# An edge sort in which GpSimd makes the maximum of half of each step's pairs

## The chip, the core and the metric

The kernel runs on one core of one Trainium2 chip. The metric is the device time of one execution in microseconds (us). The kernel before takes 11703.05 us in the median of 3 runs (11698.67 to 11715.26).

## The reference

The reference is a network of four layers on x of shape (8, 128, 64, 64): an involution (a 7x7 filter computed from the data), a mixture of 8 experts with a capacity, a 3x3 convolution, and a mixture of 4 experts whose gates come from a graph attention over 524288 random edges and one loop for each node. Only the last needs the sort:

```
src = edge_index[0] and the loops;  dst = edge_index[1] and the loops
e = leaky_relu(a_src[src] + a_dst[dst], negative_slope=0.2)
e_max = segment_max(e, dst);  ee = exp(e - e_max[dst])
denom = segment_sum(ee, dst)
agg = segment_sum(h[src] * (ee / (denom[dst] + 1e-16))[:, :, None], dst)
```

To make the segment sums into scans, the kernel first sorts the 524288 edges by destination. The key of an edge is the whole number (dst + 256) shifted left by 15, or'ed with src: the destination above, the source in the 15 bits below.

## The kernel before

`metaformer` runs its stages one after the other, each in a block of its own with a barrier at its end: the sort of the edges, the involution with the first routing, the experts, the node ranges, the convolution, the scan over the edges, and the gates with the output. Every stage starts when all engines have left the one before.

`sort_edges` (L1085 to L1234) is a bitonic sorting network. The keys lie as 128 partitions x 4096 in one of two buffers, `buf[0]` and `buf[1]`; each step reads one and writes the other, and `a` says which is read. A key is compared as the fp32 number whose bits it is, which for positive numbers orders in the same way as the whole numbers. The list `steps` (L1104 to L1112) is made beforehand and walked in order (L1188 to L1222). It has these kinds:

- "both", 66 steps (runs shorter than 4096): pairs lie `d = 1 << j` apart, and blocks go up and down by turns. Four instructions on VectorE, each on 1024 elements a partition: minimum and maximum for the blocks that go up (`e = 0`), and for those that go down (`e = 1`), where the two outputs change places (L1216, L1217).
- "rows", 124 steps (longer runs, all in one direction): two instructions on VectorE, the minimum and the maximum of all 2048 pairs (L1210, L1211).
- "sign", 8 steps: partitions that go down are multiplied by -1 (L1205, L1207).
- "turn", 14 steps: the keys are transposed in blocks on TensorE into PSUM, and ScalarE and VectorE copy them back (L1158, L1166, L1195), so that pairs that lie in different partitions come to lie in one.

After the last instruction of a step VectorE waits for the semaphore `stage` to reach the step's number (L1219 to L1221), because the next step reads what this one wrote. In a turn VectorE raises `turn_in` (L1192), for which TensorE waits. GpSimd's part of this stage is a single iota (L1145). At the end VectorE takes the keys apart into sources, destinations and a mark for equal neighbours, and SyncE stores them.

Other lines that the text speaks of: L388 is a copy on GpSimd in the involution, beside which VectorE makes one-hot rows (L204, L205); L1760 are GpSimd's indirect DMAs in the last stage, beside which VectorE multiplies and adds (L1847, L1854, L1858, L1866); L92, L94 and L739 are memsets on GpSimd.

Of the kernel before, what the change touches and what calls it, by code (L numbers as in the profile page):

```python
# [50 lines left out]
FE = NEDGE // P  # L51
# [1033 lines left out]
def sort_edges(nc, src, dst, srcs, dsts, cont, ident):  # L1085
# [3 lines left out]
    with ExitStack() as ctx:  # L1089
# [6 lines left out]
        sign = sb("sign", [P, LP + 1])  # L1096
        loaded, made, stage = sem("loaded"), sem("made"), sem("stage")
        turn_in, turn_psum, turn_act, turn_dve = sem("turn_in"), sem("turn_psum"), sem("turn_act"), sem("turn_dve")
        done, stored = sem("done"), sem("stored")


# [19 lines left out]
        def bank_dst(t, q):  # L1121
# [4 lines left out]
                return out.rearrange("p (q b) -> p b q", b=FE // P)[:, 4 * q:4 * q + 4]  # L1126
            return out.rearrange("q (b p) -> q b p", p=P)[:, 4 * q:4 * q + 4]

        block = ctx.enter_context(nc.Block())

        @block.sync
# [11 lines left out]
        @block.gpsimd  # L1143
        def _(pool):
            nc.gpsimd.iota(part[:], pattern=[[0, 1]], base=0, channel_multiplier=1).then_inc(made, 1)  # L1145

        @block.tensor
        def _(pe):
# [21 lines left out]
        def _(dve):  # L1170
# [12 lines left out]
            dve.wait_ge(stage, 3 + LP)  # L1183
            nc.vector.tensor_scalar(sign[:, 0:LP], bit[:], -2.0, 1.0, ALU.mult, ALU.add)
            nc.vector.memset(sign[:, LP:LP + 1], 1.0).then_inc(stage, 1)
            n, t, a = 4 + LP, 0, 0
            dve.wait_ge(stage, n)
            for kind, k, j in steps:  # L1188
                x, y = buf[a][:], buf[1 - a][:]
                d = 1 << j  # L1190
                if kind == "turn":
                    dve.sem_inc(turn_in, 1)  # L1192
                    for q in range(1, NTURN, 2):
                        dve.wait_ge(turn_psum, NTURN * t + q + 1)
                        nc.vector.tensor_copy(bank_dst(t, q), bank[q][:].rearrange("p (b q) -> p b q", b=4)  # L1195
                                              ).then_inc(turn_dve, 1)
                    t += 1
                    dve.wait_ge(turn_act, (NTURN // 2) * t)
                    dve.wait_ge(turn_dve, (NTURN // 2) * t)
                    a ^= 1  # L1200
                    continue
                if kind == "sign":
                    m = k - LF
                    if m == 0:
                        ins = nc.vector.tensor_scalar(y, x, sign[:, 0:1], None, ALU.mult)  # L1205
                    else:
                        ins = nc.vector.tensor_scalar(y, x, sign[:, m - 1:m], sign[:, m:m + 1], ALU.mult, ALU.mult)  # L1207
                elif kind == "rows":
                    vx, vy = (v.rearrange("p (m two d) -> p m two d", two=2, d=d) for v in (x, y))
                    nc.vector.tensor_tensor(vy[:, :, 0], vx[:, :, 0], vx[:, :, 1], ALU.min)  # L1210
                    ins = nc.vector.tensor_tensor(vy[:, :, 1], vx[:, :, 0], vx[:, :, 1], ALU.max)  # L1211
                else:
                    vx, vy = (v.rearrange("p (n e m two d) -> p n e m two d", e=2, two=2, d=d, m=1 << (k - j - 1))
                              for v in (x, y))
                    for e in range(2):
                        nc.vector.tensor_tensor(vy[:, :, e, :, e], vx[:, :, e, :, 0], vx[:, :, e, :, 1], ALU.min)  # L1216
                        ins = nc.vector.tensor_tensor(vy[:, :, e, :, 1 - e], vx[:, :, e, :, 0], vx[:, :, e, :, 1],  # L1217
                                                      ALU.max)
                ins.then_inc(stage, 1)  # L1219
                n += 1  # L1220
                dve.wait_ge(stage, n)  # L1221
                a ^= 1  # L1222
            key = fin[:].bitcast(I32)
            nc.vector.tensor_scalar(other[:].bitcast(I32), key, (1 << 15) - 1, None, ALU.bitwise_and).then_inc(done, 1)
# [6 lines left out]
            nc.vector.memset(other[:, 0:1], 0.0)  # L1231
            nc.vector.tensor_tensor(other[:, 1:FE], key[:, 1:FE], key[:, 0:FE - 1], ALU.is_equal).then_inc(done, 1)

        return loaded, made, stage, turn_in, turn_psum, turn_act, turn_dve, done, stored  # L1234


def node_ranges(nc, counts, ends, endtab, ident):
# [809 lines left out]
```

## Time and profile before

| | us |
|---|---|
| median of 3 runs | 11703.05 |
| lowest, highest | 11698.67, 11715.26 |
| the profiled execution | 11711.42 |
| its span, first to last instruction | 11709.7 |
| busy: TensorE, VectorE, ScalarE, GpSimd | 5363.1, 4831.0, 2011.8, 5292.8 |
| the sorting network, steps alone | 24.47 to 1015.10 of the span |

The profile is of one execution, on the one core. DVE is VectorE, POOL is GpSimd, ACT is ScalarE, PE is TensorE's matmuls and PEld its weight loads, SP is SyncE. A queue is named by a q behind the engine. A timeline line has the start in us from the span's start, the duration in us, the engine, the line of the kernel, the operation, output <- input and their shapes, and in brackets the engine's idle time before it with what released it. Durations of neighbours on one engine overlap a little, so the distance of two starts is the better measure of a sequence. A waiting engine whose instruction has already been handed over shows the wait as part of that instruction's duration, not as idle time.

### The profile page before, as it was taken

The page shows a single profiled execution, that of the slowest core. Times are in us where ns is not written, and L with a number is a line of the kernel's source. Part 1 is how long each engine was busy: PE and PEld are TensorE (multiplying, and loading weights), DVE is VectorE, ACT ScalarE, POOL GpSimd, SP SyncE. Part 2 cuts the span into 40 slices and gives each one's busy share as a digit, 9 for nine tenths or more (in the row PEclk, how much of TensorE's full clock was granted, in tenths as well). Part 3 has the DMA queues.
Part 4 walks back from the last instruction along what each step waited for, and adds up shares of the span by engine and source line. Part 5 has one row for each costly group of instructions (what it writes and reads, how often), then busy time and mean ns, then how long its engine had stood idle before and what let it go on. Part 6 is the DMA issues. An engine that isn't in the chain of part 4 may idle for free. (4 is left out here: it accounts for less than half of the span.)

```text
span 11709.7 us, 84534 instructions
## 1 busy us (share of the span) xinstructions
PE 5363.1 (46%) x20795; PEld 3127.3 (27%) x20795; DVE 4831.0 (41%) x13362; ACT 2011.8 (17%) x3739; POOL 5292.8 (45%) x5293
## 2 busy tenths in 40 slices
PE   0112999999978996888512112121212122121135
PEld 0111666666656772333200000000000000000012
DVE  9996666666657873434211111111111111111168
ACT  0000333333322321111011111111111111111100
POOL 0000111111110004333477777777777777777662
PEclk9755999999989998888756555565556565565568
DMA  0002000000002112332411111111111111111165
GB/s 14 0 0 101 23 23 23 22 21 21 20 19 89 57 52 51 56 58 59 51 34 36 33 36 35 35 39 31 39 32 39 33 36 34 36 39 31 39 168 190
DMA packets 382082, 514.68 MB, mean 44 GB/s; under 512 B 215894, under 2 KB 302735, under 8 KB 357139
## 3 DMA queue, kind: packets, MB, share of 16 engines
q1 hardware_dynamic: 184466, 260.41, 7.9%
q0 software_dynamic: 164992, 77.85, 6.8%
q10 hardware_dynamic: 32256, 171.98, 3.7%
q8 instruction: 175, 2.87, 0.1%
q14 instruction: 193, 1.57, 0.0%
HBM read 249.78 MB, written 263.86 MB: 44 GB/s over the span
## 5 line engine op out<-in xcount | busy, mean ns | idle before, releaser
L1501 POOL DMA_INDIRECT e_row<-rows_dram,e_idx x4096 | 4031.5, 984 | 1264.4 <-issue 1264.4
L1447 PE MATMUL e_bank<-e_hid,e_w 128*128 128x512 f32 x1024 | 592.9, 714 | 4189.1 <-ACT e_hid L1477 4189.1
L1534 DVE COPY e_idx<-e_allidx 128x64 int32 x64 | 13.2, 206 | 4353.4 <-DMA e_row<-rows_dram,e_idx 4353.4
L1447 PEld LDWEIGHTS e_bank<-e_hid,e_w 128*128 128x128 f32 x1024 | 220.7, 223 | 4492.4 <-issue 4492.4
L388 POOL COPY a_xc<-a_xp 128x1573 f32<-128x1573 f32 x104 | 167.7, 1617 | 1224.2 <-PE a_bank L441 1111.7
L205 DVE TENSOR_SCALAR a_cnta_hot<-a_cnta_iota,a_cnta_part 128x256 bf16<-128x256 bf16 x2368 | 693.1, 293 | 0.0
L1485 ACT ACTIVATE e_ex<-e_dx 128x512 f32<-128x512 f32 x64 | 40.3, 630 | 3573.7 <-DVEq L1547 3573.7
L204 DVE TENSOR_SCALAR a_cnta_hot<-a_cnta_iota,a_cnta_part 128x128 bf16<-128x128 bf16 x2368 | 649.6, 274 | 0.0
L397 POOL DMA_INDIRECT xb_dram<-a_so,a_sidx x256 | 251.4, 982 | 813.5 <-DVE a_sidx L664 548.1
L467 PE MATMUL a_bank<-a_taps,a_xt 121*128 121x100 f32 x2704 | 590.9, 360 | 2.0 <-ACT a_xt L531 2.0
L951 POOL DMA_INDIRECT v_dram<-c_td,c_fidx x256 | 251.4, 982 | 736.4 <-DVE c_td L1076 660.8
L1440 PE MATMUL e_bank<-e_h,e_w 128*128 128x512 f32 x1024 | 509.7, 627 | 67.8 <-DMA e_h<-hn_dram 67.8
L980 PE MATMUL c_bank<-c_xp,c_w 128*128 128x512 f32 x1152 | 497.8, 593 | 19.0 <-ACT c_rl L1005 19.0
L429 PE MATMUL a_bank<-a_hid,a_canvas 128*121 128x169 f32 x1600 | 484.1, 481 | 6.9 <-ACT a_hid L517 6.9
L1158 PE MATMUL s_bank<-keep_ident,s_keys 128*128 128x128 f32 x448 | 83.6, 373 | 876.0 <-DVEq L1192 876.0
L205 DVE TENSOR_SCALAR b_cntb_hot<-b_cntb_iota,b_cntb_part 128x256 bf16<-128x256 bf16 x1728 | 481.9, 279 | 0.3 <-issue 0.3
L367 POOL MEMSET a_xp<- 128x5041 f32 x1 | 4.3, 4301 | 1038.3 <-POOLq L1992 1038.3
L467 PEld LDWEIGHTS a_bank<-a_taps,a_xt 121*128 121x128 f32 x2704 | 452.8, 200 | 11.4 <-ACT a_xt L531 3.6
L204 DVE TENSOR_SCALAR b_cntb_hot<-b_cntb_iota,b_cntb_part 128x128 bf16<-128x128 bf16 x1728 | 427.3, 247 | 0.1
L212 PE MATMUL a_bank<-a_cnta_hot 128*128 128x256 bf16 x2368 | 401.6, 275 | 16.3 <-DVE a_cnta_hot L205 1.9
L1263 POOL MEMSET h_ones<- 128x128 f32 x1 | 0.2, 206 | 863.8 <-POOLq L675 863.8
L429 PEld LDWEIGHTS a_bank<-a_hid,a_canvas 128*121 128x121 f32 x1600 | 330.7, 207 | 162.9 <-ACT a_hid L517 14.2
(345 smaller groups left out, 10655.0 us busy)
## 6 DMA issues: line engine op xcount, KB each, us to landing
e_row<-rows_dram,e_idx POOLq DMA_INDIRECT x4096
ys_dram<-e_y ACTq DMA_DIRECT2D x64, 1024.0 KB, 4.0
f_ye<-ys_dram SPq DMA_DIRECT2D x64, 1024.0 KB, 4.8
res_dram<-e_st ACTq DMA_DIRECT2D x64, 768.0 KB, 3.3
xb_dram<-a_taps SPq DMA_DIRECT2D x4, 5120.0 KB, 31.1
b_tok<-xb_dram SPq DMA_DIRECT2D x80, 256.0 KB, 2.7
yb_dram<-b_y ACTq DMA_DIRECT2D x80, 256.0 KB, 2.0
x_dram<-a_xs SPq DMA_DIRECT2D x9, 2048.0 KB, 6.3
```

The lines of the kernel that those rows point to most:

```text
L204: self.nc.vector.tensor_scalar(h[:, 0:P], self.iota[:, 0:P], self.part[:, 0, c:c + 1], None, ALU.is_equal)
L205: self.nc.vector.tensor_scalar(h[:, P:], self.iota[:], self.part[:, 1, c:c + 1], None, ALU.is_equal).then_inc(self.hot_ready, 1)
L212: self.nc.tensor.matmul(self.psum, h[:, 0:P], h[:, P:], start=(c == 0), stop=(c == self.C - 1)).then_inc(self.counted, 1)
L388: nc.gpsimd.tensor_copy(xq[a % 2].rearrange("p (b r c) -> p b r c", r=IN, c=IN), bass.AP(tensor=rows.tensor, offset=rows.offset, ap=[list( ...
L397: nc.gpsimd.indirect_dma_start(xb, bass.IndirectOffsetOnAxis(ap=sidx[:, t:t + 1], axis=0), ht[:, t], None, bounds_check=SLOTS - 1, oob_is_ ...
L429: nc_mm = nc.tensor.matmul(bank[q % 4][0:KIN, (z % 3) * NP:(z % 3 + 1) * NP], canvas[:, g, at:at + KIN], hid[:, r::OUT, c::OUT], start=Tru ...
L467: mm = nc.tensor.matmul(bank[6 + v % 2][:, (b - b0) * G * NOUT:(b - b0 + 1) * G * NOUT], xt[0:KIN, u % 3, z % 4, :], taps[0:KIN, :, z], st ...
L951: nc.gpsimd.indirect_dma_start(v, bass.IndirectOffsetOnAxis(ap=fidx[:, t:t + 1], axis=0), td[:, t], None, bounds_check=NEDGE - 1, oob_is_e ...
L980: mm = nc.tensor.matmul(bank[4 + t % 2][:], w9[:, k], xp[:, 8 * t + a:8 * t + a + 8, b:b + W], start=(k == 0), stop=(k == K3 * K3 - 1))
L1440: nc.tensor.matmul(bank[m % UPB][:], w1[:, e, f * P:(f + 1) * P], h[:, s], start=True, stop=True).then_inc(up_psum, 1)
L1447: mm = nc.tensor.matmul(bank[UPB + n % DNB][:], w2[:, n % NE, f], hid[:, n % 2, f], start=(f == 0), stop=(f == NF1 - 1))
L1501: nc.gpsimd.indirect_dma_start(row[:, s, u], None, rows, bass.IndirectOffsetOnAxis(ap=idx[:, s, u:u + 1], axis=0)).then_inc(gath[s], 16)
```

## The change

The pairs of every "rows" and "both" step are cut into two halves of 1024 pairs a partition by the new function `halves`. For "both" the halves are the blocks that go up and those that go down; for "rows" they are the first and second half of the runs, or, where there is one run alone, of its elements. VectorE makes minimum and maximum of the first half as before, and the minimum alone of the second. GpSimd makes the maximum of the second half in two instructions on the keys as whole numbers: the sum of both inputs, written where the maximum belongs, and then that sum less the minimum.

Four semaphores order this. VectorE raises `input_ready` at the start of a step, and GpSimd's sum waits for it. The minimum of GpSimd's half is VectorE's first instruction of the step and raises `least_ready`. GpSimd's difference waits for its own sum (`mixed`) and for `least_ready`, and raises `maxed`. At the end of a step VectorE waits for `maxed` as well as for `stage`. Signs, turns and what comes before and after the network stay as they are.

```
--- before.py
+++ after.py
@@ -1096,6 +1096,7 @@
         sign = sb("sign", [P, LP + 1])
         loaded, made, stage = sem("loaded"), sem("made"), sem("stage")
         turn_in, turn_psum, turn_act, turn_dve = sem("turn_in"), sem("turn_psum"), sem("turn_act"), sem("turn_dve")
+        input_ready, least_ready, mixed, maxed = (sem(n) for n in ("input_ready", "least_ready", "mixed", "maxed"))
         done, stored = sem("done"), sem("stored")
 
 
@@ -1126,6 +1127,18 @@
                 return out.rearrange("p (q b) -> p b q", b=FE // P)[:, 4 * q:4 * q + 4]
             return out.rearrange("q (b p) -> q b p", p=P)[:, 4 * q:4 * q + 4]
 
+        def halves(x, k, j, kind):
+
+            d = 1 << j
+            if kind == "rows":
+                vx = x.rearrange("p (m two d) -> p m two d", two=2, d=d)
+                m = FE // (2 * d)
+                cut = [(slice(0, m // 2), slice(0, d)), (slice(m // 2, m), slice(0, d))] if m > 1 else [
+                    (slice(0, 1), slice(0, d // 2)), (slice(0, 1), slice(d // 2, d))]
+                return [[(vx[:, a, 0, b], vx[:, a, 1, b])] for a, b in cut]
+            vx = x.rearrange("p (n e m two d) -> p n e m two d", e=2, two=2, d=d, m=1 << (k - j - 1))
+            return [[(vx[:, :, e, :, 0], vx[:, :, e, :, 1])] for e in range(2)]
+
         block = ctx.enter_context(nc.Block())
 
         @block.sync
@@ -1143,6 +1156,19 @@
         @block.gpsimd
         def _(pool):
             nc.gpsimd.iota(part[:], pattern=[[0, 1]], base=0, channel_multiplier=1).then_inc(made, 1)
+            n, a = 0, 0
+            for kind, k, j in steps:
+                if kind in ("rows", "both"):
+                    n += 1
+                    pool.wait_ge(input_ready, n)
+                    (x,), (y,) = halves(buf[a][:], k, j, kind)[1], halves(buf[1 - a][:], k, j, kind)[1]
+                    least, most = (v.bitcast(I32) for v in (y[::-1] if kind == "both" else y))
+                    nc.gpsimd.tensor_tensor(most, x[0].bitcast(I32), x[1].bitcast(I32), ALU.add
+                                            ).then_inc(mixed, 1)
+                    pool.wait_ge(mixed, n)
+                    pool.wait_ge(least_ready, n)
+                    nc.gpsimd.tensor_tensor(most, most, least, ALU.subtract).then_inc(maxed, 1)
+                a ^= 1
 
         @block.tensor
         def _(pe):
@@ -1183,7 +1209,7 @@
             dve.wait_ge(stage, 3 + LP)
             nc.vector.tensor_scalar(sign[:, 0:LP], bit[:], -2.0, 1.0, ALU.mult, ALU.add)
             nc.vector.memset(sign[:, LP:LP + 1], 1.0).then_inc(stage, 1)
-            n, t, a = 4 + LP, 0, 0
+            n, t, a, pooled = 4 + LP, 0, 0, 0
             dve.wait_ge(stage, n)
             for kind, k, j in steps:
                 x, y = buf[a][:], buf[1 - a][:]
@@ -1205,20 +1231,18 @@
                         ins = nc.vector.tensor_scalar(y, x, sign[:, 0:1], None, ALU.mult)
                     else:
                         ins = nc.vector.tensor_scalar(y, x, sign[:, m - 1:m], sign[:, m:m + 1], ALU.mult, ALU.mult)
-                elif kind == "rows":
-                    vx, vy = (v.rearrange("p (m two d) -> p m two d", two=2, d=d) for v in (x, y))
-                    nc.vector.tensor_tensor(vy[:, :, 0], vx[:, :, 0], vx[:, :, 1], ALU.min)
-                    ins = nc.vector.tensor_tensor(vy[:, :, 1], vx[:, :, 0], vx[:, :, 1], ALU.max)
                 else:
-                    vx, vy = (v.rearrange("p (n e m two d) -> p n e m two d", e=2, two=2, d=d, m=1 << (k - j - 1))
-                              for v in (x, y))
-                    for e in range(2):
-                        nc.vector.tensor_tensor(vy[:, :, e, :, e], vx[:, :, e, :, 0], vx[:, :, e, :, 1], ALU.min)
-                        ins = nc.vector.tensor_tensor(vy[:, :, e, :, 1 - e], vx[:, :, e, :, 0], vx[:, :, e, :, 1],
-                                                      ALU.max)
+                    dve.sem_inc(input_ready, 1)
+                    pooled += 1
+                    px, py = halves(x, k, j, kind), halves(y, k, j, kind)
+                    nc.vector.tensor_tensor(py[1][0][kind == "both"], px[1][0][0], px[1][0][1], ALU.min
+                                            ).then_inc(least_ready, 1)
+                    nc.vector.tensor_tensor(py[0][0][0], px[0][0][0], px[0][0][1], ALU.min)
+                    ins = nc.vector.tensor_tensor(py[0][0][1], px[0][0][0], px[0][0][1], ALU.max)
                 ins.then_inc(stage, 1)
                 n += 1
                 dve.wait_ge(stage, n)
+                dve.wait_ge(maxed, pooled)
                 a ^= 1
             key = fin[:].bitcast(I32)
             nc.vector.tensor_scalar(other[:].bitcast(I32), key, (1 << 15) - 1, None, ALU.bitwise_and).then_inc(done, 1)
@@ -1231,7 +1255,7 @@
             nc.vector.memset(other[:, 0:1], 0.0)
             nc.vector.tensor_tensor(other[:, 1:FE], key[:, 1:FE], key[:, 0:FE - 1], ALU.is_equal).then_inc(done, 1)
 
-        return loaded, made, stage, turn_in, turn_psum, turn_act, turn_dve, done, stored
+        return loaded, made, stage, turn_in, turn_psum, turn_act, turn_dve, input_ready, least_ready, mixed, maxed, done, stored
 
 
 def node_ranges(nc, counts, ends, endtab, ident):
```

## Rows read from the trace of the kernel before

**Rows 1.** The page: engines (part 1), two lines of the slices (part 2).

```profile
PE 5363.1 (46%) x20795; PEld 3127.3 (27%) x20795; DVE 4831.0 (41%) x13362; ACT 2011.8 (17%) x3739; POOL 5292.8 (45%) x5293
...
DVE  9996666666657873434211111111111111111168
...
POOL 0000111111110004333477777777777777777662
```

**Rows 2.** Busy time by stretch: length, each engine's busy us, clock, DMA.

```profile
24.47:332.60 308.13, 0.00 (x0) 0.00 (x0) 305.92 (x262) 0.00 (x0) 0.00 (x0) 1.00 0.00 0
332.60:1015.10 682.50, 83.61 (x448) 80.62 (x448) 626.21 (x316) 44.59 (x56) 0.00 (x0) 0.60 0.00 0
```

**Rows 3.** Timeline (start, duration, engine, line) at the next stage's start.

```profile
1040.53 4.30 POOL L367 MEMSET a_xp<- 128x5041 f32 x1 [1038.27 <-POOLq L1992]
```

**Rows 4.** Groups by line in the sort: count, busy us, mean ns, idle before.

```profile
L1210 DVE TENSOR_TENSOR s_keys<-s_keys 128x2048 f32<-128x2048 f32 x124 | 284.2, 2292 | 5.4
...
L1216 DVE TENSOR_TENSOR s_keys<-s_keys 128x1024 f32<-128x1024 f32 x132 | 162.7, 1233 | 2.3
```

**Rows 5.** Timeline in the sort: first step, a "both" and a "rows" step.

```profile
24.47 2.00 DVE L1216 TENSOR_TENSOR s_keys<-s_keys 128x1024 f32<-128x1024 f32 x1
...
32.14 1.23 DVE L1216 TENSOR_TENSOR s_keys<-s_keys 128x1024 f32<-128x1024 f32 x1
...
36.80 1.23 DVE L1216 TENSOR_TENSOR s_keys<-s_keys 128x1024 f32<-128x1024 f32 x1
37.95 1.22 DVE L1217 TENSOR_TENSOR s_keys<-s_keys 128x1024 f32<-128x1024 f32 x1
...
41.47 1.22 DVE L1216 TENSOR_TENSOR s_keys<-s_keys 128x1024 f32<-128x1024 f32 x1
...
416.36 2.29 DVE L1210 TENSOR_TENSOR s_keys<-s_keys 128x2048 f32<-128x2048 f32 x1
...
420.89 2.29 DVE L1210 TENSOR_TENSOR s_keys<-s_keys 128x2048 f32<-128x2048 f32 x1
```

**Rows 6.** Timeline of GpSimd at the start: a wait on itself.

```profile
1.26 0.29 POOL L1982 TENSOR_SCALAR_AFFINE_SELECT keep_ident<-keep_ident 128x128 f32<-128x128 f32 x1 [0.24 <-POOL keep_ident L1980]
```

**Rows 7.** GpSimd's groups by line, and the copy's min/median/max.

```profile
L739 POOL MEMSET b_zeros<- 128x4096 f32 x1 | 3.5, 3507 | 0.0
...
L92 POOL MEMSET keep_ln_ones<- 128x128 f32 x1 | 0.2, 207 | 0.0
...
L388 POOL COPY a_xc<-a_xp x104: 1542/1612/1695, 1148.2 to 3369.4; 128x1573 f32<-128x1573 f32 x104
```

**Rows 8.** Timeline around a copy on GpSimd, and min/median/max of L204.

```profile
1229.99 1.59 DVE L204 TENSOR_SCALAR a_cnta_hot<-a_cnta_iota,a_cnta_part 128x128 bf16<-128x128 bf16 x1
...
1229.88 1.66 POOL L388 COPY a_xc<-a_xp 128x1573 f32<-128x1573 f32 x1 [6.50 <-PE a_bank L441]
...
L204 DVE TENSOR_SCALAR a_cnta_hot<-a_cnta_iota,a_cnta_part x2368: 235/242/1618, 1216.5 to 3393.2; 128x128 bf16<-128x128 bf16 x198
```

**Rows 9.** Timeline of the last stage, and min/median/max of L1760.

```profile
11331.55 1.43 POOL L1760 DMA_INDIRECT f_st<-res_dram,keep_last_i  x1 [0.30 <-issue]
...
11332.08 1.21 DVE L1847 TENSOR_TENSOR f_prod<-f_ye,f_wide 128x1024 f32<-128x1024 f32 x1
...
11333.28 2.56 POOL L1760 DMA_INDIRECT f_st<-res_dram,keep_last_i  x1 [0.30 <-issue]
...
11333.81 1.21 DVE L1854 TENSOR_TENSOR f_acc<-f_prod 128x1024 f32<-128x1024 f32 x1
...
11334.95 1.21 DVE L1847 TENSOR_TENSOR f_prod<-f_ye,f_wide 128x1024 f32<-128x1024 f32 x1
...
L1760 POOL DMA_INDIRECT f_st<-res_dram,keep_last_i x256: 940/945/2566, 11117.0 to 11561.8; - x128
```

**Rows 10.** Timeline: GpSimd released by VectorE.

```profile
1147.29 0.69 DVE L149 TENSOR_TENSOR a_xp<-a_xc,a_bank 128x512 f32<-128x512 f32 x1 [0.17 <-PE a_bank L122]
...
1148.17 1.55 POOL L388 COPY a_xc<-a_xp 128x1573 f32<-128x1573 f32 x1 [99.14 <-DVE a_xp L149]
```

## The prediction

> **What bounds the kernel now.** The page comes first: one core, GpSimd, TensorE and VectorE each busy under half of the span [rows 1], so no engine bounds the whole; the kernel is a row of stages with barriers between them. The slices of the page show which stage the change meets: in slices 0 to 2 VectorE stands at 9 tenths and GpSimd at 0 [rows 1]. The table of busy time by stretch gives the stage its edges: 24.47 to 1015.10 us is the sorting network, first 308.13 us in which VectorE alone works, then 682.50 us in which TensorE and ScalarE help at the turns; GpSimd is at 0.00 in both [rows 2]. The next stage starts on GpSimd after 1038.27 us of idle [rows 3], so what the network gains or loses moves all that follows by the same amount. Nothing after it overlaps it.
>
> Inside the network VectorE is its own bound. The groups by line show 124 "rows" steps of two instructions of 2048 elements, and 66 "both" steps of four instructions of 1024 [rows 4]. The instructions overlap a little at their ends, so I go by starts in the timeline. A "both" step takes 41.47 - 36.80 = 4.67 us, and within it one instruction follows the next by 1.14 us [rows 5]. Four times 1.14 are 4.56, so the wait between steps costs 0.11 us. A "rows" step takes 420.89 - 416.36 = 4.53 us [rows 5]. The very first step, whose elements lie 16 bytes apart, takes 32.14 - 24.47 = 7.67 us [rows 5].
>
> **The change part by part.** Of every step VectorE now issues three instructions of 1024 elements: the minimum of GpSimd's pairs, then the minimum and maximum of its own. GpSimd issues two, a sum and a difference, on 1024 elements each. The three on VectorE cost 3 x 1.14 = 3.42 us, plus the 0.11 us of the wait, plus a semaphore increment and a second wait. The trace doesn't price these two alone; they lie between nothing and GpSimd's 0.24 us for a wait on itself [rows 6], and I take 0.05 us, as they are nearer to VectorE's own wait. VectorE's share of a step is thus 3.58 us: 0.95 us less in "rows", 1.09 us less in "both".
>
> GpSimd has no two-input instruction in this trace, so its price is bounded. Its copies of 1573 elements have a median of 1612 ns [rows 7], 1.025 ns an element; a memset of 4096 takes 3507 ns [rows 7], 0.85 ns an element; one of 128 takes 207 ns, of which 0.1 us doesn't go with the elements [rows 7]. If two inputs cost no more than one, an instruction takes 1024 x 1.025 + 0.1 = 1.15 us. If each input is a pass of its own, it takes 2.2 us at the copy's rate and 1.84 us at the memset's. If the result is a third pass, it takes 3.25 us. I take 2.2 us: the copy is the nearest row, since it reads and writes as these do, and the doubled input is the one difference.
>
> The Trainium skill ("GPSIMD Engine Reference", section "Elementwise — side-by-side cycle accounting") puts a GpSimd tensor_tensor of 2048 fp32 elements at 4497 ns, because both inputs share one read port; no run here shows it. Half of it is an estimate of 2.25 us, by which the forecast below would be some 20 us later.
>
> Does GpSimd's work lie beside VectorE's, or behind it? Two sets of rows speak. First, while GpSimd copied from 1229.88 for 1.66 us, a VectorE instruction of 0.24 us in the median took 1.59 us and ended with the copy, at 1231.58 against 1231.54 [rows 8]. VectorE was held for GpSimd's whole instruction. Second, in the last stage VectorE runs two-input instructions of the same kind and size as the sort's, back to back, and GpSimd's indirect DMAs, 945 ns in the median, take 1.43 and 2.56 us [rows 9]. Each ends 0.9 us after one of VectorE's starts: 11331.55 + 1.43 is 0.90 behind 11332.08, and 11333.28 + 2.56 is 0.89 behind 11334.95 [rows 9]. GpSimd was held until a VectorE instruction gave way. What isn't shown is a two-input VectorE instruction against a GpSimd instruction that reads all the time; both halves of an exclusive hold are. So I take the step's five instructions as one queue, not two.
>
> The Trainium skill says the same of the pair that isn't shown ("SBUF — State Buffer", section "Who interferes with whom": a two-input VectorE instruction against a GpSimd read, the later one blocks entirely). By it the forecast stands; without it the no-hold rival below would have more weight.
>
> The queue has two possible orders. VectorE goes first, since GpSimd is released by a VectorE event only 0.2 us later (1148.17 against 1147.29 + 0.69) [rows 10]. If the two then take turns, the step is 3.58 + 2 x (2.2 - 0.2) = 7.58 us: the held VectorE instruction of [rows 8] ended 0.04 us after the copy though it needs 0.24 us, so 0.2 us overlap at each handover. The wait between sum and difference is covered by VectorE's instruction. If VectorE runs its three first (a waiting GpSimd let one of VectorE's starts, 11333.81, go by [rows 9]), the step is 3.42 + 2.2 + 0.24 + 2.2 + 0.11 + 0.05 = 8.22 us, with GpSimd's release of VectorE put at the 0.11 us of VectorE's wait on itself. I take the middle, 7.9 us, since the rows don't tell the order.
>
> Behind the new wait on VectorE stands the next step's whole work, and, at the 14 turns, the increment that lets TensorE begin; nobody else waits. Signs, turns and the code behind the sort are untouched and GpSimd sits idle in them. Clearing four more semaphores on SyncE costs well under 1 us.
>
> The sum: 124 x (7.9 - 4.53) = 418 us; 65 x (7.9 - 4.67) = 210 us; the first step 3 x 1.9 + 0.16 + 4.4 = 10.3 against 7.67, 3 us. Together +631 us. On the median, 11703 + 631 = **12334 us**; the profiled execution (11711.4 us, 1.7 of it around the span) would read 12342. That is 5.4% slower. A difference of 0.2%, 23 us, is about what a measurement of this kernel can tell from no change.
>
> **The rivals.**
> 1. The hold is shared element by element. Then VectorE's second inputs (3 x 1024 at 1.1 ns, 3.4 us) and GpSimd's inputs (4 x 1024 at 0.85 ns, 3.5 us) queue at one port, and the step is about 7.0 us: 124 x 2.47 + 65 x 2.33 = +458, 12161 us. For it: nothing in the rows; against it, the hold of a whole copy [rows 8].
> 2. Hold, but cheap GpSimd instructions (1.15 us): 3.58 + 2 x 0.95 = 5.48 us a step, 118 + 53, about 11874 us. No row shows a second input for nothing.
> 3. No hold between these two kinds, GpSimd's chain sets the step: 0.2 + 2.2 + 0.24 + 2.2 + 0.11 = 4.95 us, 124 x 0.42 + 65 x 0.28 - 2 = +68, 11771 us. For it: the rows that hold VectorE are of a one-input form. Against it: [rows 9], where the two-input form holds GpSimd.
> 4. The other side, faster: no hold and GpSimd hidden. VectorE's three instructions set the step at 3.58 us, 124 x 0.95 + 65 x 1.09 + 2 = 191 us off, 11512 us. It decides only if there is no hold and a GpSimd instruction takes under 2.0 us, where 0.55 + 2A passes a step of 4.57 us. With a hold, a gain would need A under 0.7 us, less than one pass over 1024 elements.
> 5. The change doesn't do what it says: the whole-number sum is rounded and the keys come out other than the maxima. The instructions and their durations stay; only the addresses of later gathers would differ. No time of its own follows; with whatever else could keep the step as it is, the result is near 11703 us.
>
> **How the numbers follow.** Full hold with two passes or more: 0.77. Shared element by element: 0.07. Hold, cheap instructions: 0.04. No hold, GpSimd's chain: 0.06. No hold, hidden: 0.03. The fifth: 0.03, mostly within 0.2%. The range: its low end is the full hold at the memset's rate, taking turns: 3.58 + 2 x 1.64 = 6.86 us, 289 + 142 + 2, about 12136 us, rounded to 12130, which takes in rival 1. Its high end is three passes, taking turns: 3.58 + 2 x 3.05 = 9.68 us, 639 + 326 + 4, 12672 us, rounded to 12670; 0.04 of the first case lies above it (three passes, VectorE first). So 0.80 lies inside. Faster by over 0.2%: 0.03; within: 0.02; slower: 0.95.
>
> **What would show each step.** Full hold: in the sort, VectorE's 1024-element instructions no longer all take 1.22 us [rows 5]; some are stretched by a GpSimd instruction, or GpSimd's are stretched by VectorE's, and the starts of a step lie 7.6 to 8.2 us apart; the network ends near 1645 us and the next stages keep their lengths. If turns are taken, the stretched ones are VectorE's second and third; if not, VectorE's three start 1.14 us apart and GpSimd's sum is the stretched one. Price of GpSimd: the shortest distance from a sum to its difference, about 2.4 us with the wait. No hold: VectorE's durations all at 1.22 us with idle time before each step, released by GpSimd (rival 3) or none (rival 4). The prediction is wrong if the step is under 6.9 or over 9.7 us, or if time moves in a stage behind the sort.

## The result and the profile after

The changed kernel takes 12309.91 us in the median of 4 runs (12297.06 to 12317.73), the kernel before 11709.15 us in the median of 4; the ratio is 1.0515, 95% interval 1.0499 to 1.0532. That is 600.8 us more, where 631 us were forecast, and 12309.91 us lies in the forecast's range of 12130 to 12670 us. The profiled execution took 12297.06 us.

The page of the changed kernel (busy time, and the slices of VectorE and GpSimd) answers to [rows 1]:

```profile
PE 5361.0 (44%) x20795; PEld 3116.0 (25%) x20795; DVE 5405.9 (44%) x13420; ACT 2011.7 (16%) x3739; POOL 6293.1 (51%) x5673
...
DVE  9999956666666578443421111111111111111168
...
POOL 6656621111111100233347777777777777777763
```

GpSimd gained 6293.1 - 5292.8 = 1000 us of busy time, VectorE 575 us, although VectorE has one quarter fewer comparisons to make. Busy time here holds the time an instruction is held, too. Busy time by stretch answers to [rows 2]; the last line is everything behind the sort:

```profile
24.50:535.98 511.48, 0.00 (x0) 0.00 (x0) 496.12 (x198) 0.00 (x0) 350.26 (x132) 1.00 0.00 0
535.98:1615.64 1079.66, 80.36 (x448) 77.37 (x448) 1008.56 (x436) 44.61 (x56) 658.78 (x248) 0.59 0.00 0
...
1641.30:12295.30 10654.00, 5280.66 (x20347) 3038.65 (x20347) 3880.34 (x12769) 1965.79 (x3682) 5283.25 (x5286) 0.74 0.19 47
```

The network now runs from 24.50 to 1615.64 us: 1591.1 us against 990.6, which is 600.5 us more, all of the difference of the medians. What lies behind it takes 10654.0 us against 10669.2 in the execution profiled before. These 15 us are within the 21 us by which the four runs of the changed kernel differ among themselves.

The groups by line in the sort (count, busy us, mean ns, idle before) answer to [rows 4]. L1238, L1240 and L1241 are VectorE's first minimum, second minimum and maximum (in the timelines below, L1166 is GpSimd's sum and L1170 its difference):

```profile
L1238 DVE TENSOR_TENSOR s_keys<-s_keys 128x1024 f32<-128x1024 f32 x190 | 622.6, 3277 | 38.2 <-DVE s_keys L1241 31.9 <-POOL s_keys L1170 4.1 <-DVE s_keys L1231 0.2
L1241 DVE TENSOR_TENSOR s_keys<-s_keys 128x1024 f32<-128x1024 f32 x190 | 614.1, 3232 | 0.0
...
L1240 DVE TENSOR_TENSOR s_keys<-s_keys 128x1024 f32<-128x1024 f32 x190 | 231.0, 1216 | 0.0
```

Two of VectorE's three have a mean over 3.2 us, the middle one 1.22 us. One step of the timeline (start and duration in us) tells why. It answers to the steps of [rows 5]; its pairs lie 1024 elements apart:

```profile
546.50 2.34 POOL L1166 TENSOR_TENSOR s_keys<-s_keys 128x1024 int32<-128x1024 int32 x1 [1.25 <-DVEq L1235]
546.52 3.40 DVE L1238 TENSOR_TENSOR s_keys<-s_keys 128x1024 f32<-128x1024 f32 x1 [0.18 <-DVE s_keys L1241]
549.84 1.21 DVE L1240 TENSOR_TENSOR s_keys<-s_keys 128x1024 f32<-128x1024 f32 x1
550.07 3.19 POOL L1170 TENSOR_TENSOR s_keys<-s_keys 128x1024 int32<-128x1024 int32 x1 [1.23 <-DVE s_keys L1238]
550.98 3.35 DVE L1241 TENSOR_TENSOR s_keys<-s_keys 128x1024 f32<-128x1024 f32 x1
554.50 2.34 POOL L1166 TENSOR_TENSOR s_keys<-s_keys 128x1024 int32<-128x1024 int32 x1 [1.25 <-DVEq L1235]
```

The sum and the first minimum begin together, and the minimum ends 1.1 us after the sum: 546.52 + 3.40 = 549.92 against 548.84. So GpSimd was first, and VectorE did its 1.1 us of work behind it. The second minimum runs alone. The difference is handed over at 550.07 while that runs, and ends 2.2 us after the second minimum: 550.07 + 3.19 = 553.26 against 549.84 + 1.21 = 551.05. The maximum, handed over at 550.98, ends 1.07 us after the difference. Then follows 0.17 us, and the next step. All five stand in one queue, and the step takes 8.00 us. Where pairs lie 1 or 2 elements apart (50 of the 190 steps, the first among them), the sum takes 1.89 us and the step 7.11 us in all but the first:

```profile
521.90 1.89 POOL L1166 TENSOR_TENSOR s_keys<-s_keys 128x1024 int32<-128x1024 int32 x1 [1.25 <-DVEq L1235]
...
529.01 1.89 POOL L1166 TENSOR_TENSOR s_keys<-s_keys 128x1024 int32<-128x1024 int32 x1 [1.25 <-DVEq L1235]
```

The first step, with elements 16 bytes apart, went in another order. VectorE's three ran first, at 2.0 us each, and the sum was held behind all three: it took 7.71 us, where the difference behind it, with nobody beside it, took 1.98 us (32.28 to 34.26):

```profile
24.50 7.71 POOL L1166 TENSOR_TENSOR s_keys<-s_keys 128x1024 int32<-128x1024 int32 x1 [22.23 <-DVEq L1235]
...
28.28 2.06 DVE L1241 TENSOR_TENSOR s_keys<-s_keys 128x1024 f32<-128x1024 f32 x1
...
34.39 1.89 POOL L1166 TENSOR_TENSOR s_keys<-s_keys 128x1024 int32<-128x1024 int32 x1
```

### The profile page after: what moved, and what is told of

Its sections match the earlier page's. It is cut to its first block and busy times, and to the rows that moved or that the text cites. A ratio compares the mean times of both kernels' runs of the same rounds, so it can differ in the third digit from the quotient of the medians.

```text
span 12295.3 us, 85351 instructions
## 1 busy us (share of the span) xinstructions
PE 5361.0 (44%) x20795; PEld 3116.0 (25%) x20795; DVE 5405.9 (44%) x13420; ACT 2011.7 (16%) x3739; POOL 6293.1 (51%) x5673
## 5 line engine op out<-in xcount | busy, mean ns | idle before, releaser
L1170 POOL TENSOR_TENSOR s_keys<-s_keys 128x1024 int32<-128x1024 int32 x190 | 581.6, 3061 | 232.4 <-DVE s_keys L1238 232.3
L204 DVE TENSOR_SCALAR a_cnta_hot<-a_cnta_iota,a_cnta_part 128x128 bf16<-128x128 bf16 x2368 | 651.6, 275 | 0.0
L1238 DVE TENSOR_TENSOR s_keys<-s_keys 128x1024 f32<-128x1024 f32 x190 | 622.6, 3277 | 38.2 <-DVE s_keys L1241 31.9
L1166 POOL TENSOR_TENSOR s_keys<-s_keys 128x1024 int32<-128x1024 int32 x190 | 427.4, 2250 | 370.8 <-DVEq L1235 370.7
L1241 DVE TENSOR_TENSOR s_keys<-s_keys 128x1024 f32<-128x1024 f32 x190 | 614.1, 3232 | 0.0
```

Source lines behind the costliest of these rows:

```text
L204: self.nc.vector.tensor_scalar(h[:, 0:P], self.iota[:, 0:P], self.part[:, 0, c:c + 1], None, ALU.is_equal)
L1166: nc.gpsimd.tensor_tensor(most, x[0].bitcast(I32), x[1].bitcast(I32), ALU.add).then_inc(mixed, 1)
L1170: nc.gpsimd.tensor_tensor(most, most, least, ALU.subtract).then_inc(maxed, 1)
L1238: nc.vector.tensor_tensor(py[1][0][kind == "both"], px[1][0][0], px[1][0][1], ALU.min).then_inc(least_ready, 1)
L1241: ins = nc.vector.tensor_tensor(py[0][0][1], px[0][0][0], px[0][0][1], ALU.max)
```

## The experiments

The theory is the exclusive hold: a VectorE instruction with two SBUF inputs and a GpSimd instruction that reads SBUF never run at once. The rivals are a port shared element by element, a GpSimd whose chain is merely too long, and a hold of any instruction by any other. The network's length, from its first instruction to the first one behind it, serves as the measure: it is the same wherever the kernel ran. The kernels e1, e2, e3 and e9 ran on a chip on which the kernel before takes 12489.28 us in one run, where the 4096 indirect DMAs of the edge stage take 1072 ns each in the mean (profiled in e2) and not 984 ns; the unchanged network of e9_gpsimd_prices took 1591.9 us on it, against 1591.1 us.

| kernel | a step, us (pairs 4 or more apart) | network, us |
|---|---|---|
| before | 4.53 and 4.67 | 990.6 |
| changed | 8.00 | 1591.1 |
| e1, VectorE alone | 3.64 | 812.0 |
| e2, one after the other | 8.42 | 1673.7 |
| e3, second input from PSUM | 4.89 | 1049.8 |
| e4, GpSimd only writes | 3.67 | 816.1 |
| e5, GpSimd copies | 5.37 | 1146.8 |
| e8, released later | 7.82 | 1564.2 |
| e7, a quarter in "rows" alone | 6.37 ("rows") | 1204.8 |
| e10, turns compared from PSUM | 4.53 and 4.67 | 944.8 |

**VectorE alone.**

```diff
-                dve.wait_ge(maxed, pooled)
```
and GpSimd's loop over the steps taken out.

> GpSimd's sum and difference and VectorE's wait for them are taken out; VectorE keeps its three instructions of a step, so the maxima of half of the pairs are not made, and the kernel goes on with the unsorted keys, of which a copy was kept. Theory, exclusive hold (a step's five instructions stand in one queue): without GpSimd, VectorE's three all take 1.22 us and a step 3.5 to 3.6 us, the network 790 to 805 us against 990.6 before and 1591.1 in the changed kernel. Rival, something of the new order of work itself (half-size instructions, strides, the semaphore increment) is dear: VectorE's instructions stay over 1.3 us or the step over 4 us even without GpSimd.

The timeline of VectorE in the network:

```profile
503.13 1.23 DVE L1229 TENSOR_TENSOR s_keys<-s_keys 128x1024 f32<-128x1024 f32 x1
...
506.77 1.22 DVE L1229 TENSOR_TENSOR s_keys<-s_keys 128x1024 f32<-128x1024 f32 x1
```

Every instruction took 1.22 us, and a step 506.77 - 503.13 = 3.64 us. So nothing in the new order of VectorE's own work is dear, and the step of 8.00 us is GpSimd's doing. The network, 812.0 us, was a little over the expectation: between two steps lie 3.64 - 3 x 1.14 = 0.22 us, not the 0.16 us of the prediction.

**One after the other.**

```diff
-                    dve.sem_inc(input_ready, 1)
                     pooled += 1
...
                 dve.wait_ge(stage, n)
+                if kind != "sign":
+                    dve.sem_inc(input_ready, 1)
                 dve.wait_ge(maxed, pooled)
```

> GpSimd's two instructions of a step are released only when VectorE's three have ended, so that nothing overlaps; all keys are sorted. Exclusive hold: overlapping had bought next to nothing, so a step grows only by the waits and handovers, from 7.1 and 8.0 us to 7.8 and 8.7 us; GpSimd's sum and difference each take 1.9 us (pairs 1 or 2 elements apart) and 2.3 us (4 or more apart) as in the changed kernel, VectorE's three 1.22 us each; network near 1720 us. Rival, shared element by element: GpSimd alone is clearly faster than 1.9 and 2.3 us (1.2 to 1.6 us), the step 6.4 to 7.2 us. Rival, GpSimd is merely dear and VectorE's long durations are waits for data: GpSimd takes 3 us alone and the step is over 9.5 us.

The timeline of a step with pairs 1024 apart:

```profile
565.91 1.22 DVE L1237 TENSOR_TENSOR s_keys<-s_keys 128x1024 f32<-128x1024 f32 x1
...
569.55 2.34 POOL L1166 TENSOR_TENSOR s_keys<-s_keys 128x1024 int32<-128x1024 int32 x1 [6.05 <-DVEq L1245]
571.96 2.34 POOL L1170 TENSOR_TENSOR s_keys<-s_keys 128x1024 int32<-128x1024 int32 x1
574.33 1.22 DVE L1237 TENSOR_TENSOR s_keys<-s_keys 128x1024 f32<-128x1024 f32 x1 [4.92 <-POOL s_keys L1170]
```

GpSimd's two take 2.34 us each with nobody beside them, just what the sum takes in the changed kernel, and VectorE's three are back at 1.22 us. The step is 574.33 - 565.91 = 8.42 us (7.53 us for pairs 1 or 2 apart), a little under the expected 8.7 and 7.8 us, and the network took 1673.7 us where some 1720 us were expected. Running the engines together had bought 0.42 us of 8.42. That is not what a port shared element by element gives, nor did GpSimd take the 3 us of the other rival.

**The second input from PSUM.**

```diff
-px[1][0][0], px[1][0][1], ALU.min
+px[1][0][0], second, ALU.min      # second: a view of a constant PSUM tile; so for all three
```
GpSimd writes its results to a tile of its own, `apart`.

> VectorE's three instructions of a step take their second input from a constant tile in PSUM in place of SBUF, so they have one SBUF input; GpSimd's two instructions have the same forms and inputs and write to a tile of their own. The keys aren't sorted; the kernel goes on with a kept copy of them. Exclusive hold through VectorE's second SBUF input: the hold is gone, VectorE's instructions all take 1.2 to 1.3 us, GpSimd's 1.9 to 2.4 us, and a step is GpSimd's chain alone, 4.3 us (pairs 1 or 2 apart) and 5.2 us (4 or more). Rival, a hold of any VectorE instruction against any on GpSimd: stretched instructions and steps of 7.1 and 8.0 us stay.

The timeline of one step with pairs 4 apart and one with pairs 2 apart (L1171 sum, L1175 difference; L1253, L1255, L1256 VectorE):

```profile
44.07 2.31 POOL L1171 TENSOR_TENSOR s_apart<-s_keys 128x1024 int32<-128x1024 int32 x1
44.08 1.22 DVE L1253 TENSOR_TENSOR s_keys<-s_keys,s_pair 128x1024 f32<-128x1024 f32 x1 [1.49 <-POOL s_apart L1175]
...
48.90 1.89 POOL L1171 TENSOR_TENSOR s_apart<-s_keys 128x1024 int32<-128x1024 int32 x1
...
50.87 2.80 POOL L1175 TENSOR_TENSOR s_apart<-s_apart,s_keys 128x1024 int32<-128x1024 int32 x1
...
53.80 1.89 POOL L1171 TENSOR_TENSOR s_apart<-s_keys 128x1024 int32<-128x1024 int32 x1
```

VectorE's three start 1.14 us apart and take 1.22 us beside a sum of 2.31 us. The hold is gone, and the second SBUF input is what made it. The steps, 4.83 and 4.90 us, are GpSimd's chain alone (over all pairs 4 or more apart the median is 4.89 us). This is close to the prediction's third rival (4.95 us), which would have held if the two engines could run together. Both expected steps were missed. The 5.2 us for pairs 4 or more apart were 0.3 us too long. The 4.3 us for close pairs were too short, because the difference now takes 2.80 us there; its inputs lie in two tiles in this kernel, which is the likely reason, but no run varied that alone.

**GpSimd only writes, and GpSimd copies.** Two kernels, in which the sum and the difference become

```diff
+                    nc.gpsimd.memset(most, 0.0)             # e4, twice
+                    nc.gpsimd.tensor_copy(most, x[0])       # e5, then x[1]
```

> GpSimd's sum and difference are each replaced by a memset of the same 1024 elements, which reads nothing; waits and releases stay, VectorE's three instructions have two SBUF inputs as in the changed kernel. The keys aren't sorted; the kernel goes on with a kept copy. Hold by the shared reading: a memset isn't held and holds nobody; VectorE's instructions stay at 1.22 us, memsets at 0.95 us, the step at VectorE's own 3.64 us as without GpSimd. Rival, hold of any instruction by any: the memsets queue with the rest, step 3.64 + 2 x 0.95 - 0.3 = 5.2 us, with VectorE's instructions stretched to over 2 us.

> GpSimd's sum and difference are each replaced by a copy of one input, 1.07 us alone (1.11 with elements 2 apart). The keys aren't sorted; the kernel goes on with a kept copy. Exclusive hold, one queue: the changed kernel's steps fit 3.64 + 2A - 0.3 with A the price of a GpSimd instruction alone (1.89: 7.12; 2.34: 8.02), so with A = 1.07 the step is 5.5 us. Rival, the hold comes from GpSimd's two inputs and a one-input read shares the port: step 3.64 us with VectorE's durations at 1.22 us or a little more.

A step of the one with memsets:

```profile
556.16 0.95 POOL L1167 MEMSET s_keys<- 128x1024 f32 x1 [1.34 <-DVEq L1238]
556.19 1.22 DVE L1241 TENSOR_TENSOR s_keys<-s_keys 128x1024 f32<-128x1024 f32 x1 [0.17 <-DVE s_keys L1244]
...
559.83 0.95 POOL L1167 MEMSET s_keys<- 128x1024 f32 x1 [1.35 <-DVEq L1238]
```

The memsets take 0.95 us beside VectorE's 1.22 us, and nobody is held: 3.67 us a step against 3.64 without GpSimd. A step of the one with copies:

```profile
572.97 1.04 POOL L1167 COPY s_keys<-s_keys 128x1024 f32<-128x1024 f32 x1 [1.22 <-DVEq L1238]
573.00 2.09 DVE L1241 TENSOR_TENSOR s_keys<-s_keys 128x1024 f32<-128x1024 f32 x1 [0.18 <-DVE s_keys L1244]
...
576.14 2.05 DVE L1244 TENSOR_TENSOR s_keys<-s_keys 128x1024 f32<-128x1024 f32 x1
578.34 1.04 POOL L1167 COPY s_keys<-s_keys 128x1024 f32<-128x1024 f32 x1 [1.22 <-DVEq L1238]
```

Here the stretched instructions are back, with the first minimum at 2.09 us and the maximum at 2.05. The step is 5.37 us (5.46 us for close pairs), where 5.5 us were expected. So one read by GpSimd is enough, and a write is not. The Trainium skill says both ("SBUF — State Buffer", section "Who interferes with whom"), and both runs agree.

**Released later.**

```diff
-                    dve.sem_inc(input_ready, 1)
...
                     nc.vector.tensor_tensor(..., ALU.min).then_inc(least_ready, 1)
+                    dve.sem_inc(input_ready, 1)
```

> VectorE raises input_ready behind its first minimum in the program and not before it; all keys are sorted. Engines take turns at the port: GpSimd's sum, released a little later, now finds the first minimum under way and is let in either at once behind it or as before, and the step stays one queue, 7.1 and 8.0 us within 0.15 us. Rival, a VectorE that runs back to back keeps the port, as it did through the first step of the changed kernel, where the sum ended only after all three (7.71 us): the sum starts after VectorE's third, and the step takes 7.5 and 8.4 us, as with nothing overlapped.

The timeline of a step (L1237, L1240, L1241 VectorE):

```profile
549.90 1.22 DVE L1237 TENSOR_TENSOR s_keys<-s_keys 128x1024 f32<-128x1024 f32 x1
550.01 3.31 POOL L1166 TENSOR_TENSOR s_keys<-s_keys 128x1024 int32<-128x1024 int32 x1 [1.23 <-DVEq L1239]
551.04 3.36 DVE L1240 TENSOR_TENSOR s_keys<-s_keys 128x1024 f32<-128x1024 f32 x1
...
557.72 1.23 DVE L1237 TENSOR_TENSOR s_keys<-s_keys 128x1024 f32<-128x1024 f32 x1
```

Now the first minimum runs undisturbed, the sum comes in at once behind it (550.01 + 3.31 = 553.32, 2.2 us after the minimum's end), and the second minimum is the stretched one. So in this step a VectorE that runs back to back doesn't keep GpSimd out. The step is 7.82 us, 0.18 us less than in the changed kernel and a little outside the 0.15 us expected: the idle 0.18 us before VectorE's first instruction has gone. The network is 26.9 us shorter. The one execution took 12308.26 us, so this doesn't show in the total.

**A quarter for GpSimd, in "rows" steps alone.**

```diff
-                cut = [(slice(0, m // 2), slice(0, d)), (slice(m // 2, m), slice(0, d))] if m > 1 else [
+                cut = [(slice(0, m * 3 // 4), slice(0, d)), (slice(m * 3 // 4, m), slice(0, d))] if m > 3 else [
...
```
and the "both" steps as in the kernel before.

> GpSimd gets a quarter of the pairs in place of a half, and only in the 124 rows steps; the 66 both steps are those of the kernel before. All keys are sorted. Exclusive hold: GpSimd's instructions of 512 elements take 1.3 us (1.0 to 1.1 where the pairs are 1 or 2 apart), VectorE's three (512, 1536, 1536) some 3.95 us plus 0.22; the step is 4.17 + 2 x 1.3 - 0.3 = 6.5 us (5.9), worse than 4.53 before, and the network 1205 to 1225 us against 990.6 before: a smaller share only loses less. Rival, GpSimd loses by its chain being longer than VectorE's work: with a quarter, that chain of about 3 us fits behind VectorE's, and the step is 4.2 us, the network near 950 us, faster than before.

A step of the timeline:

```profile
350.59 1.26 POOL L1166 TENSOR_TENSOR s_keys<-s_keys 128x512 int32<-128x512 int32 x1 [1.78 <-DVEq L1242]
350.61 1.79 DVE L1245 TENSOR_TENSOR s_keys<-s_keys 128x512 f32<-128x512 f32 x1 [0.18 <-DVE s_keys L1248]
...
352.54 2.64 POOL L1170 TENSOR_TENSOR s_keys<-s_keys 128x512 int32<-128x512 int32 x1 [0.69 <-DVE s_keys L1245]
...
356.96 1.26 POOL L1166 TENSOR_TENSOR s_keys<-s_keys 128x512 int32<-128x512 int32 x1 [1.78 <-DVEq L1242]
```

GpSimd needs only 1.26 us for its sum, its whole chain would fit behind VectorE's 4.2 us, and still the step takes 356.96 - 350.59 = 6.37 us (5.93 us for close pairs), against 4.53 before. The execution took 11922.10 us beside 11703.22 for the kernel before. A smaller share loses less and gains nothing, which settles it against the rival of a chain that is merely too long.

**GpSimd's prices.** A row of instructions ahead of the network, while VectorE waits:

```diff
+            for d in (1, 2, 4, 8, 64, 1024):
+                run(lambda: tt(pairs(k1, d)[0], *pairs(k0, d), ALU.add))
+                run(lambda: tt(pairs(f1, d)[0], *pairs(f0, d), ALU.add))
```

> The changed kernel, with a row of GpSimd instructions ahead of the network while VectorE waits, each form twice: whole-number and fp32 sums of 1024 pairs that lie 1, 2, 4, 8, 64 and 1024 elements apart; sums with the second input 1025, 1026 and 0 elements behind the first; sums of 512 and 2048; copies and a memset of 1024. Exclusive hold: the sums cost alone what they cost in the network, 1.9 us at 1 and 2 apart and 2.3 us from 4 on, and so whatever sets these two prices is GpSimd's own and not VectorE's doing; a copy 1.1 us, a memset 0.95 us; the very first sum takes some 6 us more, as the first of the network did (7.71 us). Rival, shared: the sums are under 1.6 us alone, and both prices alike.

GpSimd's timeline; each line holds two instructions and the time of both. The first two are whole-number sums of pairs 1 and 4 apart (those 1024 apart took 4.75 us), then come a second input 1025 elements behind the first, the same input twice, and sums of 512 and of 2048:

```profile
9.24 3.86 POOL L1179 TENSOR_TENSOR s_bench<-s_bench 128x1024 int32<-128x1024 int32 x2
...
25.00 4.77 POOL L1179 TENSOR_TENSOR s_bench<-s_bench 128x1024 int32<-128x1024 int32 x2
...
63.60 4.07 POOL L1181 TENSOR_TENSOR s_bench<-s_bench 128x1024 int32<-128x1024 int32 x2
...
71.90 3.86 POOL L1183 TENSOR_TENSOR s_bench<-s_bench 128x1024 int32<-128x1024 int32 x2
75.83 2.60 POOL L1184 TENSOR_TENSOR s_bench<-s_bench 128x512 int32<-128x512 int32 x2
78.51 9.06 POOL L1185 TENSOR_TENSOR s_bench<-s_bench 128x2048 int32<-128x2048 int32 x2
```

Alone a sum takes 3.86 / 2 = 1.93 us (1 apart, and 2 apart alike) or 2.38 us (4 and 1024 apart), so both prices are GpSimd's own. The very first pair of sums took no longer than the fp32 pair behind it, 3.86 us too, so the expected 6 us for a first one were wrong: the 7.71 us of the first step were a hold, which its timeline above shows. The network behind it is the same code as the changed kernel's, and yet its first step went another way: GpSimd's sum was first, and its difference was the one that waited.

```profile
104.05 1.98 POOL L1197 TENSOR_TENSOR s_keys<-s_keys 128x1024 int32<-128x1024 int32 x1 [9.98 <-DVEq L1267]
104.06 3.77 DVE L1270 TENSOR_TENSOR s_keys<-s_keys 128x1024 f32<-128x1024 f32 x1 [0.15 <-DVE s_sign L1243]
...
107.98 5.53 POOL L1201 TENSOR_TENSOR s_keys<-s_keys 128x1024 int32<-128x1024 int32 x1 [1.95 <-DVE s_keys L1270]
```

**Turns compared straight from PSUM, without GpSimd.** As PSUM inputs cost VectorE nothing extra in e3, this one changes the kernel before: ScalarE copies the second key of each pair, and VectorE takes the first from the bank.

```diff
-                        nc.vector.tensor_copy(bank_dst(t, q), ...)
+                        nc.vector.tensor_tensor(y0, x0, z, ALU.min)
+                        nc.vector.tensor_tensor(y1, x0, z, ALU.max)
```

> The kernel before, without any work on GpSimd, and with the 14 turns changed: where it copied the transposed keys from PSUM and then ran a rows step on them, ScalarE now copies only the second key of each pair (256 elements a bank) and VectorE makes minimum and maximum straight from PSUM and that copy, 16 instructions of 256 elements a turn. All keys are sorted. What the runs so far show of the hold (one input from PSUM costs VectorE the same 1.22 us for 1024 elements and TensorE and ScalarE hold nobody) gives: a turn and the step behind it now take some 8.4 + 4.53 = 12.9 us; then 16 instructions at 0.35 to 0.4 us, 5.6 to 6.4 us, behind 2.5 us of start-up, 8 to 9 us; 14 x 4 to 5 = 55 to 70 us less, 0.5 to 0.6% faster than before. Rival, short instructions with strided PSUM inputs are dear (0.5 us or more each): a turn takes as long as before, within 0.2%.

A turn (L1173 TensorE, L1212 and L1213 VectorE from PSUM, L1226 the next step):

```profile
402.36 3.71 PE L1173 MATMUL s_bank<-keep_ident,s_keys 128*128 128x128 f32 x32 [2.08 <-DVEq L1208]
...
403.46 0.61 DVE L1212 TENSOR_TENSOR s_keys<-s_bank,s_second 128x256 f32<-128x256 f32 x1 [1.21 <-ACT s_second L1182]
...
410.69 2.29 DVE L1226 TENSOR_TENSOR s_keys<-s_keys 128x2048 f32<-128x2048 f32 x1
```

It takes 12549.78 us in the median of 6 runs, beside 12597.97 us in the median of 9 for the kernel before, measured with it (both are longer than above; in e10's profile the edge stage's indirect DMAs take 1077 ns each). The ratio is 0.9963 (0.9951 to 0.9976), so it is 0.4% faster than the kernel before, and beats both kernels; 0.5 to 0.6% were expected. The network is 45.8 us shorter, not 55 to 70. The turn with its step takes the expected 8.3 us, but those of before took 11.6 us in the mean and not 12.9: (990.6 - 124 x 4.53 - 65 x 4.67 - 7.67 - 8 x 2.4) / 14 + 4.53. Hence 3.3 us a turn and not 4 to 5.

## Why the prediction was right, step by step

- *The sort is a stage of its own, and what it loses the kernel loses.* Right: 600.5 us in the network, 600.8 us in the medians.
- *The five instructions are one queue.* Right, and shown from several sides: GpSimd's prices don't change when nothing runs beside it (e2, e9), the hold goes with VectorE's second SBUF input (e3) or with GpSimd's reading (e4), and comes back with a single read (e5). The two halves seen before, [rows 8] and [rows 9], did add up to the whole.
- *VectorE's share 3.58 us.* 3.64 us (e1); the second wait and the increment cost 0.11 us, not 0.05.
- *GpSimd's instruction 2.2 us.* The mean was right and no single one was: 1.89 us in the 50 close steps (1.98 us in the first of them), 2.34 us in 140, which is 2.22 us in the mean. Two passes at the copy's rate was the right bound to take, but that it hit the mean to 0.02 us was luck, since the forecast knew nothing of two prices. The Trainium skill's 4497 ns for 2048 elements ("GPSIMD Engine Reference", section "Elementwise — side-by-side cycle accounting") agrees with 9.06 / 2 = 4.53 us in e9; the forecast by it would have been 20 us further off.
- *The order, and so 7.9 us for the step.* Here a term was off. I let VectorE go first, by the 0.2 us of [rows 10]; GpSimd's sum went first, 0.01 to 0.02 us ahead, since its release stands in VectorE's queue before the first minimum. The two then took turns in all but the first step, so the middle between turns (7.58) and no turns (8.22) was too high. With the measured parts, turns give 3.64 + 2A less 0.32 us (two handovers at 0.16 us, not 0.2): 7.10 us at 1.89, 8.00 us at 2.34, which are the measured steps. The steps as timed, 140 at 8.00, 49 at 7.11 and the first at 9.9 us, add up to 1478 us, where the forecast had 189 x 7.9 + 10.3 = 1503 us. These 25 us are most of the 30 by which the forecast missed; the rest lies outside these steps, in what it took as unchanged. That it came so close is partly luck, for two errors of opposite sign met: the middle lay 0.32 us above the order that came true, and the parts of that order were 0.18 us too small (VectorE's share 0.06, GpSimd's two 0.04, the handovers 0.08). With turns alone the forecast would have been 571 us, as far off on the other side.
- *The first step 10.3 us.* It took 34.39 - 24.50 = 9.9 us.
- *The stretched instructions.* I named VectorE's second and third; they were the first and third, for the same reason as the order. When the release was moved behind the first minimum (e8), it was the second and third.
- *The rivals.* Sharing (7.0 us) fell with e2; cheap instructions with e9; no hold with the step itself, though e3 shows what it would have given. The fourth was drawn too wide: for the step to be 3.58 us, a GpSimd instruction would have to take under (3.58 - 0.55) / 2 = 1.5 us, not 2.0. The way to a gain wasn't open at any share of the work that was tried (e7).

One reading of the rows was off, though its conclusion stands. In [rows 9] I took L1847 for an instruction of the sort's kind, but its second input, `f_wide`, lies in PSUM. These two lines of the kernel before belong beside it:

```profile
11331.48 0.68 DVE L1858 TENSOR_TENSOR f_acc<-f_acc 128x512 f32<-128x512 f32 x1
...
11333.21 0.68 DVE L1866 TENSOR_TENSOR f_xo<-f_xo,f_acc 128x512 f32<-128x512 f32 x1
```

GpSimd's indirect DMAs were held by VectorE instructions with both inputs in SBUF. The first ended at 11332.98, 0.82 us behind the end of L1858 (11331.48 + 0.68), and the second at 11335.84, 0.82 us behind the end of L1854 (11333.81 + 1.21), both while L1847 was running. Eleven indirect DMAs of that stage that were handed over while L1847 ran took less than 1 us, as alone. So the trace of before already showed what e3 showed later for GpSimd's sums.

What stays open is what decides when a waiting engine is let in. In all steps of the changed kernel but the first it came in at the first boundary between two instructions. In the first step, whose elements lie 16 bytes apart, VectorE kept GpSimd waiting to the end of its last instruction: the sum took 7.71 us here and 7.52 us in e8, the difference 5.53 us in e9 and GpSimd's second copy 5.54 us in e5. That it is GpSimd's first step isn't the reason, for in e7 GpSimd's first step, with pairs far apart, took 6.38 us like the others. The 16 bytes can't be the whole reason either: the second DMA above waited through L1866 and then through L1854 as well. No run varied this alone.

## What to carry to other kernels

Before giving half of a VectorE loop to GpSimd, ask what each instruction reads. If VectorE's has two SBUF inputs and GpSimd's reads SBUF, add both engines' durations, as if they were one engine. At 2.3 us against 1.1 us for 1024 elements, and two instructions for one, no split pays; that is an estimate from these durations, and the half (8.00 us a step) and the quarter (6.37 us) that were tried bear it out.

What ran beside VectorE without a hold was TensorE (L1854 takes 1.21 us beside matmuls as without them), GpSimd's memsets (e4), and GpSimd's sums once VectorE took its second input from PSUM (e3). ScalarE ran beside an instruction with two SBUF inputs too seldom to say more than that three of L1858, 0.68 us each, were no longer for it. A single SBUF input isn't always enough: in [rows 8] a VectorE instruction with one tensor input, on bf16, was held by GpSimd's copy, and no run here took that form apart.

The trace of the old kernel had both halves of the hold in other stages. To find such a thing, look for an instruction whose duration has a maximum several times its median, and at what the other engine did at that moment.

## What the runs showed of the hardware

- GpSimd's two-input price depends on how far apart the inputs lie. For 1024 elements: 1.93 us for the same input twice or pairs 1 or 2 elements apart, 2.04 us for an input 1025 elements behind, 2.38 us for 4 or 1024 elements apart (e9), and 2.80 us and more for pairs 1 or 2 apart with the two inputs in different tiles (e3). Two dense inputs are not the cheap case here. Sums of 512 and 2048 elements took 1.30 and 4.53 us. With elements 16 bytes apart a sum took 1.98 us, against 1.89 us at 8 bytes (e2).
- Whole-number sums cost GpSimd what fp32 sums cost: 3.86 us for two of either kind (e9).
- VectorE's minimum of 1024 elements takes 1.22 us with the second input in PSUM (e3), as with it in SBUF. With elements 16 bytes apart in SBUF it takes 2.0 us (first step).
- In e10 instructions of 256 elements took 0.42 us in some turns and 0.6 us in others.
